# Unread dense products on TensorE around the strips that build the spline weights

## The chip, the cores and the metric

The kernel runs on one core of one Trainium2 chip. The metric is the device time of one execution in microseconds (us); the kernel before took 2858.16 us, the median of three runs (2856.34 to 2862.82). Five engines work side by side and meet at semaphores: TensorE (PE in the profile, PEld for its weight loads), VectorE (DVE), ScalarE (ACT), GpSimd (POOL) and SyncE (SP), which issues the transfers.

## The reference

The reference is a small network of four layers over x of shape 8 x 100 x 512 with a context of 8 x 361 x 512. Each layer adds a cross attention and a feed-forward part to x, each on the layer-normed x. What matters here is the feed-forward part of the second layer:

```
w = 0.5 * (2.0 * p1 + (p2 - p0) * f + (2.0 * p0 - 5.0 * p1 + 4.0 * p2 - p3) * f2 + (3.0 * p1 - p0 - 3.0 * p2 + p3) * f3)
...
gate = jnp.einsum('bsh,ih->bsi', hidden_states, gate_w)
up = jnp.einsum('bsh,ih->bsi', hidden_states, up_w)
inter = jax.nn.silu(gate) * up
return jnp.einsum('bsi,hi->bsh', inter, down_w)
```

Its three weights (2048 x 512, 2048 x 512 and 512 x 2048) are not given. Each is interpolated by the cubic in the first line from about 8100 control points p, where f is how far a weight lies between two of them.

## The kernel before, in words

The stages follow one another, with a barrier of all engines and a clearing of semaphores between them (`end_stage`). The stage concerned, `stage_L1_ffn` (from L2400), first builds the three weights in one tile of SBUF, `w`, 128 x 24576 fp32, and then calls `stage_columns_ffn`, which runs the feed-forward part with them. Inside the stage each block of engine programs also ends at a barrier, so nothing of the second block starts before the first is done.

A weight is a cubic in its place within a run of 128 weights, so 128 weights of one run are a product of 20 coefficients (points times powers) and a fixed matrix of 20 x 128 (`terms`). Some runs cross a control point: beyond it the second of two such matrices holds, so every run is computed from both (`side` 0 and 1) and the second is laid over the first under a mask.

The weights are made in 12 parts (`PARTS_W`) of 2048 columns (`PARTW`), each in N = 4 strips of 512. Strip n of a part lies on partitions 32n to 32n + 19 of the tiles `points` and `terms`, that is, in a row quarter of TensorE's array of its own. The loops of the engines:

- SP (L2419 to L2429) loads the terms, then for each part points, powers (both 128 x 512 fp32) and the mask (128 x 2048 bytes), in three buffers.
- POOL (L2435) multiplies points by powers, once for each part, and counts `multiplied`.
- TensorE (L2439 to L2448) waits for `multiplied`, then runs for side 0 and side 1 the four strips, each a product of 20 rows by 128 columns of weights with 512 moving columns in fp32, into bank 4 side + n of PSUM. An fp32 product stands as two records in the trace, so there are 12 x 2 x 4 = 96 products and 192 records. From the second part on each product first waits for its bank to be emptied (`laid` for side 0, `w_made` for side 1).
- ACT (L2455) copies the four banks of side 0 into `w`.
- DVE (L2464) writes the four banks of side 1 over them under the mask.

`k.identb` is a bf16 identity of 128 x 128, and `k.zero` a tile of zeros of 128 x 512 fp32; both are made in the first stage.

Of the kernel before, what the change touches and what calls it, by code (L numbers as in the profile page):

```python
# [8 lines left out]
BF16 = mybir.dt.bfloat16  # L9
# [7 lines left out]
B, S, D = 8, 100, 512  # L17
# [27 lines left out]
class Core:  # L45
# [22 lines left out]
    def sb(self, name, shape, dt=F32, ctx=None):  # L68
        return (ctx or self.ctx).enter_context(self.nc.sbuf_tensor(name, shape, dt))

    def sem(self, name):
        assert name not in self.names
        self.names.add(name)
        self.stage_sems.append(self.nc.alloc_semaphore(name))
        return self.stage_sems[-1]
# [2325 lines left out]
def stage_L1_ffn(k, points, powers, beyond, terms, raw, rounded, early, recurrence):  # L2401


    nc = k.nc
    N = PARTW // D
    with ExitStack() as ctx:
        sem = lambda name: k.sem("s1_" + name)
        w = k.sb("s1_w", [P, PARTS_W * PARTW], F32, ctx)
        with ExitStack() as tmp:
            sb = lambda name, shape, dt=F32: k.sb("s1_" + name, shape, dt, tmp)  # L2410
            tm = sb("terms", [P, 2, P])
            pts, pw = [sb(f"points{i}", [P, D]) for i in range(3)], [sb(f"powers{i}", [P, D]) for i in range(3)]
            past = [sb(f"beyond{i}", [P, PARTW], mybir.dt.uint8) for i in range(3)]
            c_in, p_in, b_in = sem("constants_in"), [sem(f"part_in{i}") for i in range(3)], [sem(f"beyond_in{i}") for i in range(3)]
            multiplied, made, laid, w_made = sem("multiplied"), [sem(f"made{side}") for side in range(2)], sem("laid"), sem("w_made")
            with nc.Block() as block:

                @block.sync
                def _(sp):  # L2419
                    sp.dma_start(tm[:], terms).then_inc(c_in, 16)  # L2420
                    for t in range(PARTS_W):
                        i = t % 3
                        if t >= 3:
                            sp.wait_ge(made[1], N * (t - 2))
                        sp.dma_start(pts[i][:], points[t]).then_inc(p_in[i], 16)
                        sp.dma_start(pw[i][:], powers[t]).then_inc(p_in[i], 16)
                        if t >= 3:
                            sp.wait_ge(w_made, N * (t - 2))
                        sp.dma_start(past[i][:], beyond[t]).then_inc(b_in[i], 16)  # L2429

                @block.gpsimd
                def _(pool):
                    for t in range(PARTS_W):
                        pool.wait_ge(p_in[t % 3], (t // 3 + 1) * 32)
                        pool.tensor_tensor(pts[t % 3][:], pts[t % 3][:], pw[t % 3][:], ALU.mult).then_inc(multiplied, 1)  # L2435

                @block.tensor
                def _(pe):
                    pe.wait_ge(c_in, 16)  # L2439
                    for t in range(PARTS_W):  # L2440
                        pe.wait_ge(multiplied, t + 1)
                        for side, emptied in ((0, laid), (1, w_made)):
                            for n in range(N):
                                if t > 0:
                                    pe.wait_ge(emptied, (t - 1) * N + n + 1)
                                rows = slice(32 * n, 32 * n + TERMS)
                                nc.tensor.matmul(k.bank[N * side + n][:], tm[rows, side, :], pts[t % 3][rows, :],
                                                 start=True, stop=True).then_inc(made[side], 1)  # L2448

                @block.scalar  # L2450
                def _(act):
                    for t in range(PARTS_W):
                        for n in range(N):
                            act.wait_ge(made[0], t * N + n + 1)
                            act.copy(w[:, t * PARTW + n * D:t * PARTW + (n + 1) * D], k.bank[n][:]).then_inc(laid, 1)  # L2455

                @block.vector
                def _(dve):
                    for t in range(PARTS_W):
                        dve.wait_ge(b_in[t % 3], (t // 3 + 1) * 16)  # L2460
                        for n in range(N):
                            dve.wait_ge(made[1], t * N + n + 1)
                            dve.wait_ge(laid, t * N + n + 1)
                            dve.copy_predicated(w[:, t * PARTW + n * D:t * PARTW + (n + 1) * D],  # L2464
                                                past[t % 3][:, n * D:(n + 1) * D], k.bank[N + n][:]).then_inc(w_made, 1)

        third = PARTS_W * PARTW // 3
        part = lambda i: w[:, i * third:(i + 1) * third]
        stage_columns_ffn(k, "f1", part(0).rearrange("p (c n) -> p c n", c=KC),
                          part(1).rearrange("p (c n) -> p c n", c=KC), part(2).rearrange("p (c n) -> p c n", c=FC),  # L2470
                          raw, rounded, early, recurrence)
# [874 lines left out]
```

## Time and profile before

| | us |
|---|---|
| median of three runs | 2858.16 |
| the profiled execution | 2863.05 |
| its span, from the first to the last instruction | 2861.3 |
| TensorE busy in the span | 2499.0 (87%) |
| VectorE, ScalarE, GpSimd busy | 1415.8, 790.1, 785.4 |
| mean granted TensorE clock, share of full | 0.931 |

The profile shows one execution. Its page has the busy time of each engine and the span cut into 40 slices, with the TensorE clock that was granted in each in tenths of full speed; full is 2.4 GHz, and 0.5 is the lower level, 1.2 GHz. Other views group instructions by source line, list them in order of time, or give the busy time of each engine in a chosen stretch. Matmuls are pipelined, so a record lasts longer than the time by which it keeps the next one back; the distance from start to start tells the latter. A few records are missing from the trace.

### The profile page before, as it was taken

How to read it: one execution, taken by the hardware profiler on the slowest of the kernel's cores; microseconds unless marked ns; L12 is line 12 of the kernel's file. 1: busy time of each engine (PE TensorE's matmuls, PEld its weight loads, DVE VectorE, ACT ScalarE, POOL GpSimd, SP SyncE). 2: the span in 40 equal slices, each digit the busy share in tenths (PEclk: the TensorE clock that was granted, in tenths of full speed). 3: DMA queues.
4: the chain of work that ended last, by engine and by line, in shares of the span. 5: the costliest groups of instructions: out<-in, count | busy, mean ns of one | idle time of the engine just before them, and what ended most of it. 6: DMA issues, size and time to landing. Idle time of an engine off the chain costs nothing. (4 is left out here: it accounts for less than half of the span.)

```text
span 2861.3 us, 31862 instructions
## 1 busy us (share of the span) xinstructions
PE 2499.0 (87%) x10777; PEld 1334.4 (47%) x10798; DVE 1415.8 (49%) x3520; ACT 790.1 (28%) x2052; POOL 785.4 (27%) x754
## 2 busy tenths in 40 slices
PE   7999999979899946999789898799968889883998
PEld 3445555544466533555465555444423444441444
DVE  4543332033112324555567676776643554456886
ACT  1134443112111112555430101311102443433332
POOL 3654443112100032111123333200001545450333
PEclk9999999989899977999869999999988999986999
DMA  5024000021465532000142223400023000003000
GB/s 168 1 73 150 15 18 1 0 84 37 150 228 200 205 96 69 26 26 16 44 152 88 88 88 132 134 5 4 8 84 126 11 22 11 11 1 141 5 8 12
DMA packets 73777, 195.79 MB, mean 68 GB/s; under 512 B 14234, under 2 KB 23866, under 8 KB 70942
## 3 DMA queue, kind: packets, MB, share of 16 engines
q1 hardware_dynamic: 67486, 180.78, 18.3%
q0 software_dynamic: 6144, 13.13, 1.6%
q8 instruction: 83, 1.36, 0.2%
q14 instruction: 64, 0.52, 0.1%
HBM read 150.32 MB, written 38.60 MB: 66 GB/s over the span
## 5 line engine op out<-in xcount | busy, mean ns | idle before, releaser
L3095 POOL TENSOR_SCALAR a_p<-a_p,a_li 100x257 f32<-100x257 f32 (+1 forms) x256 | 187.1, 752 | 179.1 <-DVE a_li L2992 179.1
L632 POOL TENSOR_SCALAR a_shared<-a_shared,a_li 128x361 f32<-128x361 f32 x104 | 131.8, 1267 | 203.1 <-DVE a_li L537 203.1
L2289 PE MATMUL bank<-f_xT,s_w 128*128 128x400 f32 x512 | 181.6, 509 | 1.3 <-ACT f_xT L2313 1.3
L1908 PE MATMUL bank<-s_wgu,f_xT 128*128 128x512 f32 x384 | 168.9, 593 | 0.7 <-ACTq L2083 0.7
L1378 PE MATMUL bank<-a_ctx,w_wk 128*128 128x361 f32 x256 | 89.2, 494 | 66.1 <-PEq L117 57.1
L2289 PEld LDWEIGHTS bank<-f_xT,s_w 128*128 128x128 f32 x512 | 99.3, 194 | 78.4 <-issue 6.4
L1908 PE MATMUL bank<-s_w,f_xT 128*128 128x512 bf16 x564 | 129.6, 384 | 5.7 <-POOLq L2050 5.1
L1198 POOL DMA_INDIRECT c_got<-slots_y,slots_of x32 | 37.0, 1158 | 288.7 <-SPq L1174 279.3
L1908 PEld LDWEIGHTS bank<-s_wgu,f_xT 128*128 128x128 f32 x384 | 72.7, 190 | 92.2 <-issue 90.5
L334 PE MATMUL bank<-a_wv,a_ctx 128*128 128x512 f32 (+1 forms) x192 | 94.6, 614 | 8.2 <-DMA a_wv<-in_L_xattn_Wv 8.2
L2781 PE MATMUL bank<-a_wv,a_ctx 128*128 128x512 f32 (+1 forms) x192 | 98.9, 663 | 2.8 <-DVE a_pt L2997 2.7
L334 PE MATMUL bank<-a_wk,a_ctx 128*128 128x512 f32 (+1 forms) x192 | 93.9, 610 | 7.0 <-DMA a_ctx<-in_ctxT 7.0
L2781 PE MATMUL bank<-a_wk,a_ctx 128*128 128x512 f32 (+1 forms) x192 | 90.2, 613 | 3.6 <-DVE a_pt L2997 3.6
L1378 PEld LDWEIGHTS bank<-a_ctx,w_wk 128*128 128x128 f32 x256 | 48.3, 198 | 93.3 <-issue 62.1
L1908 PEld LDWEIGHTS bank<-s_w,f_xT 128*128 128x128 bf16 x576 | 56.8, 99 | 74.4 <-POOLq L2050 4.9
L2298 PE MATMUL bank<-f_h,s_w 128*128 128x400 f32 x256 | 90.9, 499 | 0.0
L1664 POOL TENSOR_TENSOR a_prod<-a_ctx,a_row_weights 128x1444 f32<-128x1444 f32 x8 | 24.0, 3000 | 242.0 <-DVE ctx_sum L1537 236.7
L409 PE MATMUL bank<-a_q_o,a_wq_wo 128*128 128x400 f32 x256 | 88.4, 500 | 0.6 <-issue 0.6
L1091 PE MATMUL bank<-e_wd,e_midT 128*128 128x512 f32 (+1 forms) x192 | 87.9, 593 | 0.6 <-ACT e_midT L1128 0.6
L1386 PE MATMUL bank<-w_wv,a_ctx 128*128 128x512 f32 (+1 forms) x192 | 87.2, 598 | 0.0
L681 ACT ACTIVATE a_shared<-a_shared,a_nm 128x361 f32<-128x361 f32 x104 | 62.1, 597 | 90.0 <-DVE a_nm L531 90.0
L349 PE MATMUL bank<-a_wq_wo,a_shared 128*128 128x512 f32 x192 | 86.5, 593 | 0.0
(412 smaller groups left out, 5103.1 us busy)
## 6 DMA issues: line engine op xcount, KB each, us to landing
f_triple<-in_L_ffn_triples SPq DMA_DIRECT2D x16, 768.0 KB, 4.1
rounded<-f_triple SPq DMA_DIRECT2D x16, 768.0 KB, 3.3
l_triple<-rounded SPq DMA_DIRECT2D x16, 768.0 KB, 6.2
s_whole_w<-in_L_ffn_w SPq DMA_DIRECT2D x3, 4096.0 KB
a_ctx<-in_ctxT SPq DMA_DIRECT2D x16, 722.0 KB
e_wg<-in_L_ffn_w_gate SPq DMA_DIRECT2D x16, 704.0 KB, 4.9
e_wu<-in_L_ffn_w_up SPq DMA_DIRECT2D x16, 704.0 KB, 6.4
slots_x<-zero SPq DMA_DIRECT2D x4, 2304.0 KB, 16.4
```

Of the source, the lines that this page charges most:

```text
L334: mm = nc.tensor.matmul(R.bank(name, b, c)[0:m, :], cx[:, kc, lo:lo + m], w[:, kc, :], start=(kc == 0), stop=(kc == KC - 1))
L349: mm = nc.tensor.matmul(bank[:], xnT[:, kc, t * P:(t + 1) * P], wq[:, kc, n * D:(n + 1) * D], start=(kc == 0), stop=(kc == KC - 1))
L409: mm = nc.tensor.matmul(R.bank("y", half, m)[:, 0:BY_HALF * S], wo[:, h, m * P:(m + 1) * P], qo[:, half * BY_HALF:(half + 1) * BY_HALF, h, ...
L632: pool.tensor_scalar(p[s % NP], p[s % NP], li[:, b % 2, h:h + 1], None, ALU.mult).then_inc(normed, 1)
L1091: mm = nc.tensor.matmul(b_y[:], midT[u % 2][0:n, c, :], wd[e % 2][0:n, c, :], start=(c == 0), stop=(c == len(IC) - 1))
L1378: mm = nc.tensor.matmul(R.bank("k", b, n)[:, 0:T], wks[:, kc, n * P:(n + 1) * P], cx[b % 2][:, kc, :], start=(kc == 0), stop=(kc == KC - 1))
L1386: mm = nc.tensor.matmul(R.bank("v", b, c)[0:m, :], cx[b % 2][:, kc, lo:lo + m], wvs[:, kc, :], start=(kc == 0), stop=(kc == KC - 1))
L1908: mm = nc.tensor.matmul(banks[u % 2][:], xT[i % 2][:, n, kc, :], w[:, kc, j * D:(j + 1) * D], start=(kc == 0 and n == 0), stop=(kc == KC - ...
L2289: mm = nc.tensor.matmul(banks[f % 2][:, 0:GT], w[:, kc, f * P:(f + 1) * P], xT[:, kc, :], start=(kc == 0), stop=(kc == KC - 1))
L2298: mm = nc.tensor.matmul(b_y[d][:, 0:GT], down[:, f - 1, d * P:(d + 1) * P], h[(f - 1) % 2][:], start=(f == 1), stop=(f == FC))
L2781: mm = nc.tensor.matmul(bank[0:m, :], columns[:, kc], w[:, kc, :], start=(kc == 0), stop=(kc == KC - 1))
L3095: pool.tensor_scalar(p[g % 2][j][:, lo:hi], p[g % 2][j][:, lo:hi], li[:, h, i:i + 1], None, ALU.mult) \
```

## The change

TensorE's program of the first block gains products whose results nobody reads: the bf16 identity as weights, and the zero tile, read as bf16, as 512 moving columns. Each uses all 128 rows and 128 columns of the array. Fourteen go to bank 0 before the first wait of the block. Then, in each part and on each side, one goes to the bank of strip 0 ahead of strip 0 and one to the bank of strip 1 ahead of strip 1, both after the wait for that bank; the strip then overwrites it. That makes 14 + 12 x 2 x 2 = 62 added products. Nothing else is touched.

```
+                    def idle(bank):
+                        nc.tensor.matmul(bank[:], k.identb[:], k.zero[:].bitcast(BF16)[:, 0:D], start=True, stop=True)
+
+                    for _ in range(14):
+                        idle(k.bank[0])
                     pe.wait_ge(c_in, 16)
                     for t in range(PARTS_W):
                         pe.wait_ge(multiplied, t + 1)
                         for side, emptied in ((0, laid), (1, w_made)):
                             for n in range(N):
                                 if t > 0:
                                     pe.wait_ge(emptied, (t - 1) * N + n + 1)
+                                if n < 2:
+                                    idle(k.bank[N * side + n])
                                 rows = slice(32 * n, 32 * n + TERMS)
                                 nc.tensor.matmul(k.bank[N * side + n][:], tm[rows, side, :], pts[t % 3][rows, :],
                                                  start=True, stop=True).then_inc(made[side], 1)
```

## Rows read from the trace of the kernel before

**Rows 1.** The page: TensorE's busy time, and the granted clock in 40 slices.

```profile
PE 2499.0 (87%) x10777; PEld 1334.4 (47%) x10798; DVE 1415.8 (49%) x3520; ACT 790.1 (28%) x2052; POOL 785.4 (27%) x754
...
PEclk9999999989899977999869999999988999986999
```

**Rows 2.** By stretch: length, PE, PEld, DVE, ACT, POOL busy (records); clock, DMA share, GB/s.

```profile
1417.00:1465.90 48.90, 42.95 (x192) 34.15 (x192) 29.50 (x47) 24.64 (x48) 15.29 (x12) 0.50 0.61 197
1484.00:1486.40 2.40, 2.40 (x5) 1.33 (x4) 0.00 (x0) 0.00 (x0) 0.00 (x0) 0.50 0.00 0
1486.40:1490.00 3.60, 3.60 (x12) 1.96 (x11) 0.33 (x1) 0.50 (x1) 0.00 (x0) 0.99 0.00 0
```

**Rows 3.** In order of time, 1400 to 1480 us: start, length, instruction, records.

```profile
1417.69 0.34 SPq L2420 DMA_DIRECT2D s_terms<-in_spline_terms  x1
...
1422.88 42.95 PE L2447 MATMUL bank<-s_points,s_terms 20*128 20x512 f32 x192 [8.52 <-POOL s_points L2435]
...
1467.36 0.80 SPq L2245 DMA_DIRECT2D f_triple<-in_L_ffn_triples  x2
```

**Rows 4.** By line, 1415 to 1470 us: records, busy us, mean ns, idle before.

```profile
L2447 PE MATMUL bank<-s_points,s_terms 20*128 20x512 f32 x192 | 42.9, 1068 | 8.5 <-POOL s_points L2435 8.5
...
L2464 DVE COPY_PREDICATED s_w<-s_beyond,bank 128x512 f32<-128x512 uint8 x48 | 30.7, 719 | 19.8 <-PE bank L2447 19.8
L2455 ACT COPY s_w<-bank 128x512 f32<-128x512 f32 x48 | 24.6, 599 | 33.6 <-PE bank L2447 33.6
L2435 POOL TENSOR_TENSOR s_points<-s_points,s_powers 128x512 f32<-128x512 f32 x12 | 15.3, 1274 | 65.4 <-DMA s_powers<-in_spline_powers 65.4
```

**Rows 5.** In order of time, PE, three short windows that end after four, eight, twelve records.

```profile
1422.88 1.24 PE L2447 MATMUL bank<-s_points,s_terms 20*128 20x512 f32 x4 [8.52 <-POOL s_points L2435]
...
1422.88 2.09 PE L2447 MATMUL bank<-s_points,s_terms 20*128 20x512 f32 x8 [8.52 <-POOL s_points L2435]
...
1422.88 2.94 PE L2447 MATMUL bank<-s_points,s_terms 20*128 20x512 f32 x12 [8.52 <-POOL s_points L2435]
```

**Rows 6.** In order of time: bf16 products of 512 columns, the clock at 0.50, then 1.00.

```profile
1412.42 1.95 PE L1400 MATMUL bank<-w_qT,a_oqT 128*100 128x512 bf16 x4 [0.46 <-DVE a_oqT L1594]
...
2653.55 2.75 PE L1908 MATMUL bank<-s_w,f_xT 128*128 128x512 bf16 x12
```

**Rows 7.** In order of time, PE: full rows, quarter rows, full rows; clock 1.00, then 0.50.

```profile
2257.18 0.59 PE L2781 MATMUL bank<-a_wk,a_ctx 128*128 128x512 f32 x1
...
2257.71 0.87 PE L2847 MATMUL bank<-a_kT,a_qT 32*100 32x361 f32 x8
2258.50 0.30 PE L2857 MATMUL bank<-ident,a_p 100*128 100x100 f32 x1
...
2194.35 1.59 PE L2847 MATMUL bank<-a_kT,a_qT 32*100 32x361 f32 x3
2195.88 0.43 PE L2857 MATMUL bank<-ident,a_p 100*128 100x100 f32 x1
```

**Rows 8.** By line: shortest, median, longest record of the quarter-row products, ns.

```profile
L2447 PE MATMUL bank<-s_points,s_terms x192: 1052/1056/1217, 1422.9 to 1464.8; 20*128 20x512 f32 x192
...
L1429 PE MATMUL bank<-a_kT,a_qT x240: 462/488/543, 1135.8 to 1399.2; 32*100 32x361 f32 x120
```

**Rows 9.** By stretch, as rows 2, where the clock falls in the first attention.

```profile
1120.00:1124.60 4.60, 3.95 (x16) 1.28 (x14) 0.54 (x5) 0.97 (x2) 0.00 (x0) 1.00 0.13 19
1124.60:1128.10 3.50, 3.33 (x19) 2.01 (x20) 3.50 (x24) 3.13 (x11) 0.00 (x0) 0.99 0.49 187
1128.10:1131.50 3.40, 3.40 (x9) 2.08 (x9) 2.60 (x7) 3.06 (x11) 0.00 (x0) 0.50 0.01 2
```

**Rows 10.** By line and form, PE, 1124.6 to 1128.1 us.

```profile
L1429 PE MATMUL bank<-a_kT,a_qT 32*100 32x361 f32 x8 | 2.2, 502 | 0.8 <-DVE a_nm L1571 0.8
L1438 PE MATMUL bank<-ident,a_p 100*128 100x100 f32 x8 | 1.4, 280 | 0.1
L1438 PE MATMUL bank<-ident,a_p 100*105 100x100 f32 x3 | 0.8, 256 | 0.0
```

More of the change, by code:

```diff
@@ L2438, in _, with idle @@
                 def _(pe):
+                    def idle(bank):
+                        nc.tensor.matmul(bank[:], k.identb[:], k.zero[:].bitcast(BF16)[:, 0:D], start=True, stop=True)
+                    for _ in range(14):
+                        idle(k.bank[0])
                     pe.wait_ge(c_in, 16)
@@ L2445, in _ @@
                                     pe.wait_ge(emptied, (t - 1) * N + n + 1)
+                                if n < 2:
+                                    idle(k.bank[N * side + n])
                                 rows = slice(32 * n, 32 * n + TERMS)
```

## The prediction, made before the kernel was run

> **What bounds the kernel now.** I read the page first: TensorE is busy in 87% of the span, and among its clock tenths is one valley of 7 and 8 around the middle [rows 1]. The table by stretch then shows what lies there. From 1417.0 to 1465.9 us, the whole block that builds the spline weights, the granted clock is 0.50, 1.2 GHz, although TensorE has 42.95 us of work in it. It is still 0.50 at 1484 us and becomes full, 2.4 GHz, only at 1486.4, after a few us of full-array products without a pause in the next block [rows 2]. In order of time: the first transfer is issued at 1417.69, the strips run from 1422.88 to 1465.83 without a hole, and the next block's first transfer goes out at 1467.36 [rows 3].
>
> Within the block TensorE sets the pace. By line, per part (twelfths of the busy times), DVE needs 2.56 us, ACT 2.05, POOL 1.28, and DVE and ACT both sit idle for TensorE (19.8 and 33.6 us) [rows 4]. TensorE's own rate is in the three short windows: the first four records fit in 1.24 us, eight in 2.09, twelve in 2.94 [rows 5]. So records come in groups of four, one for each row quarter, side by side, and a group follows the last by 0.85 us: 2 x 512 column passes at 1.2 GHz (0.853). A part is 16 records, four groups, 3.41 us, and 12 parts are 41 us of the 42.95. The rest is the wait for the second part's inputs. The block is bound by TensorE's clock and lives on four strips sharing the array.
>
> **The change, part by part.** The fourteen products ahead of the first wait: TensorE can begin them about when SP issues its first transfer, 1417.7. A bf16 product of 512 columns is one pass, 0.427 us at 1.2 GHz (half of the 0.853 above; four in 1.95 us with the drain of the last agree) and about 0.215 at 2.4 (twelve in 2.75 us with one drain) [rows 6]. 14 x 0.427 = 6.0 us would end at 1423.7; the strips could start at 1422.88 [rows 3]. With the clock rising on the way they end between 1422.7 and 1423.7, so I take 0.3 us of delay and bounds of 0 and 0.9. The cover is the wait of 8.5 us for POOL [rows 3].
>
> The 48 products between the strips cost more than their own time, and this decides the forecast. A full-array product needs all four row quarters. The one for bank 1 stands between strip 0 and strip 1. It can't start before strip 0 has left quarter 0, and strip 1 can't start before it has passed. So a side is no longer two groups of four records but: dense product, strip 0 alone (two records in a row), dense product, strips 1 to 3 together (two groups). That is 4 strip steps for each side in place of 2, 8 for a part in place of 4.
>
> Going from full to quarter rows and back is not free either. At full clock a full product of 2 x 512/2.4 = 0.427 us at 2257.18 is followed by quarter-row strips at 2257.71, 0.53 later; the eight strip records, 2 x 361/2.4 x 2 = 0.60 us of columns, are followed by a full product at 2258.50, 0.79 later [rows 7]. So in costs 0.10 and in plus out some 0.29. Of this about 0.08 is the first strip records being longer (543 against 462 ns [rows 8]): their weights are not loaded ahead. For 128 columns of weights in place of 100 I scale this to 0.10, and for the bf16 weights on the way out I add 0.02 to 0.10. That makes 0.315 us for each strip group, in and out. At half clock the last strip record keeps the full product back: it ends at 2195.94, 0.80 us after its start for 0.60 of columns, and the next starts 0.07 before that end [rows 7]; 0.13 of loss. The first spline record after a wait takes 1217 ns against 1056 [rows 8], 0.16. So in is 0.13 + 0.16, out 0.13 + 0.03, together 0.45.
>
> The Trainium skill's page "TensorEngine Tiling (Array Packing)", section "Key Properties", says that changing the tiling mode, and not only the tile, drains the engine. By that rule these switches cost something in every part, and the trace agrees (0.53 us where 0.427 would do). Without such a cost the sum below would be some 22 us smaller at half clock.
>
> Per part, at half clock: 4 x 0.43 + 8 x 0.853 + 4 x 0.45 = 1.7 + 6.8 + 1.8 = 10.3 us. At full clock: 4 x 0.215 + 8 x 0.427 + 4 x 0.315 = 0.9 + 3.4 + 1.3 = 5.5 us. Before: 3.4. Even at full clock the changed loop is the slower one. DVE's 2.56 us and ACT's 2.05 lie inside either; POOL and the transfers too.
>
> **Which clock.** The fourteen products are full-array and have no pause, as the work before the rise at 1486.4 [rows 2], so I expect the clock to rise at or shortly before the first strip. Then it has to be held. What costs it is not idleness alone: from 1124.6 to 1128.1 us TensorE is busy in 3.33 of 3.50 us at full clock, with quarter-row strips and short 100-row transposes, and the next stretch is at 0.50 [rows 9]. How thin that work is can be counted: 8 x 0.30 us on 32 rows and 11 x 0.083 us on 100 rows [rows 10] feed all 128 rows for the equivalent of 0.6 + 0.7 = 1.3 us in 3.5, or 0.38. And 43 us of strips alone (four times 20 rows, no hole) never lift it [rows 2]. The changed loop at full clock feeds 4 x 0.215 us on 128 rows and 16 x 0.427 on 20, together 0.86 + 1.07 = 1.93 us in 5.5, or 0.35: as thin as the stretch that lost it. At half clock it is 1.7 + 2.1 = 3.8 in 10.3, and nothing so thin is seen to raise it: the strips alone, 16 x 0.853 on 20 rows in 3.4 us, did not. So I take 8 us at full clock, through the end of the opening products and the first part or so, and half clock for the rest. Bounds: 3 and 16 us.
>
> **The sum.** 12 x 10.3 = 124; in 8 us at full clock 1.45 parts get done that would take 15 us, so 7 off; 0.3 for the late start; minus the 42.95 of before: 124 - 7 + 0.3 - 43 = +74 to +75 us. The rest of the program is unchanged and starts later; when the clock rises in the next block (19 us after the first one's end [rows 2, 3]) may shift by 1 or 2 us either way. Against the profiled execution's 2863.05 us, 2861.3 of it span, this is 2937.5. That execution lies 4.9 above the median of 2858.16, so beside the median I forecast 2933. Bounds for this case: no switch cost at all, 12 x 8.5 - 8 - 43 = +51; switches as dear as the whole weight load and drain, 0.75 each, 12 x 11.5 - 7 - 43 = +88. A cost below nothing is excluded, since strip 0 and the product behind it want the same rows. Own range: 2909 to 2946.
>
> **Rivals.**
>
> The clock holds. The same serial order at full clock throughout: 12 x 5.5 = 66 - 43 = +23, 2881. For it: stretches nearly as thin (0.38) are close by, and if the switches cost only 0.1 the loop feeds the rows for more of its time. Against it: the counts above. The Trainium skill, "TensorE: Matmul & The Clock Gate", section "Why this matters for your kernels", knows only idle gaps between bursts as what throws the clock back; with no such gap in the loop it would give this rival. Rows 9 speak against the rule, since there a busy engine lost the clock.
>
> The faster side: the strips keep sharing the array and the clock is full. This decides if a dense product takes only its own 0.2 us and strip 1 starts beside strip 0. TensorE would need 1.7 + 0.9 = 2.6 us a part, level with DVE's 2.56, so the block would take about 31 us and the start-up 2 more: -10, 2848. For it: strips do run side by side. Against it: between full and quarter-row products I find no overlap in the order of time [rows 7].
>
> The clock never rises, zeros as operand not counting as work: 124 - 43 + 1 = +82, 2940. For it: no row of before has a product of zeros. Against it: nothing shows that the values matter.
>
> No change: strips share the array and the dense products' 1.7 us a part at half clock are made up by some parts at full clock. It needs two errors at once.
>
> **Chances.** Forecast 0.68, the clock holds 0.13, it never rises 0.11, faster 0.05, no change 0.03. The range 2876 to 2948 takes in the forecast's own range, the holding clock and the one that never rises. A change under 0.2% (5.7 us) can't be told from none; faster 0.05, same 0.03, slower 0.92.
>
> **What would show it.** In the changed trace: records of strip 0 alone between dense ones, strips 1 to 3 in threes; ACT's copies of one bank and then three; a part every 10 us; ACT and DVE idle for TensorE for 80 us and more; 14 records before the first strip. The clock at 1.00 for some us around the first strip, then 0.50 to the end of the block. Wrong if the block lasts under 40 us (sharing kept), or if the clock stays at 1.00 and a part takes 5.5 us (first rival), or if a part at half clock takes 8.5 (switches free).

## The result

| | median us | ratio to before, 95% interval |
|---|---|---|
| before (six runs beside it) | 2857.25 | |
| changed kernel (six runs) | 2932.49 | 1.0259 (1.0241 to 1.0276) |

The change makes the kernel slower by 75.2 us. The forecast was 2933 us, +74 to +75. The profiled execution of the changed kernel took 2937.72 us, its span is 2936.0, 74.7 longer than the span before.

By stretch, the profile after (columns as in rows 2): the clock is at the lower level through nearly all of the opening products, at full for 6.8 us around the first part, and low again to the end of the block and beyond.

```profile
1415.80:1421.00 5.20, 5.12 (x13) 1.79 (x14) 0.00 (x0) 0.00 (x0) 1.02 (x1) 0.50 0.76 239
1421.00:1427.80 6.80, 6.80 (x26) 2.06 (x24) 1.50 (x3) 2.15 (x4) 2.78 (x3) 1.00 0.50 187
1427.80:1538.30 110.50, 110.49 (x219) 26.27 (x217) 28.45 (x43) 23.64 (x44) 11.38 (x9) 0.50 0.21 64
1538.30:1557.60 19.30, 7.09 (x22) 4.70 (x23) 9.61 (x26) 4.53 (x6) 1.67 (x1) 0.50 0.57 223
1557.60:1561.00 3.40, 3.40 (x11) 1.90 (x10) 0.00 (x0) 0.00 (x0) 0.00 (x0) 1.00 0.00 0
```

In the third of these stretches TensorE is busy in 110.49 of 110.50 us, and the share of the transfers has fallen from 0.61 [rows 2] to 0.21. By line, 1415 to 1545 us, the answer to rows 4: DVE and ACT do the same 48 pieces each, in 31.9 and 25.8 us (30.7 and 24.6 before), but wait 93.6 and 104.2 us for TensorE.

```profile
L2456 PE MATMUL bank<-s_points,s_terms 20*128 20x512 f32 x192 | 95.2, 1089 | 0.0
L2442 PE MATMUL bank<-zero,identb 128*128 128x512 bf16 x62 | 33.7, 589 | 3.4 <-PEq L80 3.4
L2473 DVE COPY_PREDICATED s_w<-s_beyond,bank 128x512 f32<-128x512 uint8 x48 | 31.9, 715 | 93.6 <-PE bank L2456 93.6
L2464 ACT COPY s_w<-bank 128x512 f32<-128x512 f32 x48 | 25.8, 592 | 104.2 <-PE bank L2456 104.2
```

In order of time, the start of the block (compare rows 3 and 5): first transfer, opening products, and then one side in the new order at full clock: two records of strip 0 alone, one dense product (a product over all rows and columns), six records of strips 1 to 3. The fifteen records of the second line are the fourteen and the loop's first. The strips of the second part begin at 1427.26.

```profile
1415.84 0.34 SPq L2420 DMA_DIRECT2D s_terms<-in_spline_terms  x1
...
1415.88 5.92 PE L2442 MATMUL bank<-zero,identb 128*128 128x512 bf16 x15 [3.38 <-PEq L80]
...
1421.73 1.12 PE L2456 MATMUL bank<-s_points,s_terms 20*128 20x512 f32 x2
...
1422.79 0.39 PE L2442 MATMUL bank<-zero,identb 128*128 128x512 bf16 x1
...
1423.11 1.13 PE L2456 MATMUL bank<-s_points,s_terms 20*128 20x512 f32 x6
...
1427.26 1.52 PE L2456 MATMUL bank<-s_points,s_terms 20*128 20x512 f32 x2
```

The same pattern deep in the block, at half clock, in order of time: from the dense product at 1500.02 to the one at 1505.11 is one side of 5.09 us, so a part takes 10.2.

```profile
1500.02 0.61 PE L2442 MATMUL bank<-zero,identb 128*128 128x512 bf16 x1
1500.56 2.08 PE L2456 MATMUL bank<-s_points,s_terms 20*128 20x512 f32 x6
1502.57 0.61 PE L2442 MATMUL bank<-zero,identb 128*128 128x512 bf16 x1
1503.11 2.07 PE L2456 MATMUL bank<-s_points,s_terms 20*128 20x512 f32 x2
1505.11 0.61 PE L2442 MATMUL bank<-zero,identb 128*128 128x512 bf16 x1
```

The strips run from 1421.73 to 1538.29 us, 116.6 in place of 42.95: +73.6 of the 74.7 us between the two spans.

### The profile page after: what moved, and what is told of

The parts are those of the page before. It is cut to its first block and busy times, and to the rows that moved or that the text cites. A ratio compares the mean times of both kernels' runs of the same rounds, so it can differ in the third digit from the quotient of the medians.

```text
span 2936.0 us, 32007 instructions
## 1 busy us (share of the span) xinstructions
PE 2580.1 (88%) x10860; PEld 1329.9 (45%) x10860; DVE 1417.3 (48%) x3520; ACT 790.3 (27%) x2052; POOL 784.3 (27%) x754
## 5 line engine op out<-in xcount | busy, mean ns | idle before, releaser
L1198 POOL DMA_INDIRECT c_got<-slots_y,slots_of x32 | 36.1, 1128 | 288.7 <-SPq L1174 279.2
L2456 PE MATMUL bank<-s_points,s_terms 20*128 20x512 f32 x192 | 95.2, 1089 | 0.0
```

## The experiments

Ten kernels ran, each beside the kernel before. "Block" is from the first strip record's start to the last one's end in the profiled execution (42.95 before, 116.6 changed), and the clock is that of the block. The ratio is that of the measurement and not the quotient of the two medians.

| kernel | median us | before us | ratio (95%) | block us, clock |
|---|---|---|---|---|
| loop_only | 2934.74 | 2856.01 | 1.0281 (1.0266 to 1.0296) | 121.8, half |
| both_first | 2856.55 | 2856.01 | 1.0002 (0.9994 to 1.0011) | 41.7, full |
| open_only | 2853.93 | 2856.01 | 0.9993 (0.9983 to 1.0003) | 40.4, full for 11, then half |
| ahead_of_strip0 | 2854.44 | 2856.01 | 1.0002 (0.9985 to 1.0019) | 39.3, full |
| both_first_no_open | 2890.09 | 2856.11 | 1.0124 (1.0102 to 1.0145) | 70.8, half |
| quarter_two | 2862.30 | 2856.11 | 1.0012 (0.9989 to 1.0034) | 47.6, full for 10, then half |
| quarter_all | 2849.70 | 2856.11 | 0.9981 (0.9968 to 0.9994) | 35.6, full |
| side0_only | 2866.43 | 2856.11 | 1.0025 (1.0008 to 1.0042) | 50.6, full for 6, then half |
| quarter_all_no_open | 2865.95 | 2855.77 | 1.0040 (1.0020 to 1.0059) | 51.7, half |
| quarter_all_gap | 2849.64 | 2855.77 | 0.9982 (0.9972 to 0.9992) | 36.1, full |

**Does the loss hang on the dense products or on their place?** Two kernels without the opening products, so both at half clock and both with the same 48 dense products. loop_only leaves them where the change has them:

```
-                    for _ in range(14):
-                        idle(k.bank[0])
```

> Without the 14 opening products; the 48 in the loop stay. Theory: the block begins at half clock and the loop is too thin to lift it, so every part takes the 10.18 us that the trace of the changed kernel shows at half clock: 122 us in place of 43, +79, 2936, some 4 to 6 us above the changed kernel. Rival (the loop's dense products lift the clock by themselves): a part of 5.5 us, +25. Rival (the opening products give nothing): equal to the changed kernel.

both_first_no_open puts the two of a side ahead of strip 0:

```
-                                if n < 2:
-                                    idle(k.bank[N * side + n])
+                            if t > 0:
+                                pe.wait_ge(emptied, (t - 1) * N + 2)
+                            for n in range(2):
+                                idle(k.bank[N * side + n])
```

> Both loop products of a side ahead of strip 0, as in both_first, and no opening products. Beside loop_only this is the same 48 products at the same half clock; only the place of the second one on each side differs. Theory: a part takes 4 x 0.427 + 4 x 0.853 + 2 x 0.41 = 5.9 us, the block 71 and a little: +28 to +30, 2885. The difference to loop_only, 4.2 us a part, is then the strip step and the pair of switches that standing between strips costs. Rival (all of the loss is from the dense products as such): the same as loop_only, +79. Rival (this denser loop lifts the clock by itself): 0 to +5, like both_first.

By their blocks both came as the theory has it. By stretch, the block of loop_only and the block of both_first_no_open:

```profile
1421.34:1543.11 121.77, 119.89 (x235) 29.03 (x239) 29.94 (x45) 25.80 (x48) 13.91 (x11) 0.50 0.21 67
```

```profile
1419.40:1490.20 70.80, 70.78 (x239) 15.37 (x238) 27.97 (x44) 24.64 (x48) 13.95 (x11) 0.50 0.36 112
```

The clock and the strips are the same, and 51 us lie between the two, 4.25 a part. In order of time, both_first_no_open has two dense products and then all eight records together, a side every 2.99 us:

```profile
1460.24 1.03 PE L2442 MATMUL bank<-zero,identb 128*128 128x512 bf16 x2
1461.21 2.09 PE L2456 MATMUL bank<-s_points,s_terms 20*128 20x512 f32 x8
1463.23 1.03 PE L2442 MATMUL bank<-zero,identb 128*128 128x512 bf16 x2
```

So of the 79 us that the loop products cost at half clock, 51 come from the place of the second one of each side, between strips, and 28 from the dense work and one pair of switches a side (a switch is the step from full rows to a quarter or back). By medians the difference is less, 44.65 us, and both_first_no_open is 34.0 above before where +28 to +30 were expected. Its four runs lie between 2884 and 2897 with the profiled one at the low end. The two longest have the lowest mean granted clock, 0.928 and 0.926 against 0.930, so they spent more time at half clock somewhere; no profile shows where.

loop_only against the changed kernel gives the worth of the opening products there: 5.2 us by the blocks, 3.5 by the medians, each beside its own before.

**The same with the opening products.** both_first keeps the 14 and has the loop products ahead of strip 0.

> The same 62 added products, but on each side both stand ahead of strip 0, so that the four strips follow one another again. Theory (the order costs the sharing of the array): a side is two products, one way in, two record groups, one way out: at full clock 0.43 + 0.85 + 0.31 = 1.6 us, 3.2 us a part, and 12 parts 38 us against 43 before. The array's rows are fed 0.86 + 1.07 of 3.2 us, nearly twice as densely as in the changed kernel, so the clock holds: about -4 us, 2853. If the clock falls all the same, a part takes 1.7 + 3.4 + 0.8 = 5.9 us and the block 71: +27. Rival (the work of the dense products or their writes to PSUM is what costs, wherever they stand): near the changed kernel, +60 to +80.

Right in its main point: 62 dense products, nothing lost against before, and 76 us less than the changed kernel with the same products in another place. The clock was full through the block, so a part of the 76 us is the clock and not the order; the order alone, at one clock, is in the pair above. The size was off: the block took 41.7 us, not 38, and the gain of 4 us did not come.

**No dense products in the loop.** open_only deletes the two lines of the loop.

> The 14 opening products alone, none in the loop. Theory: the clock rises with them and strips keep sharing the array, so a part at full clock takes TensorE 1.7 us and the block is DVE's, 2.6 us a part. But TensorE then waits for the second and third part's inputs, thin work; I expect the clock to fall there and the rest to run as before: -1 to -3 us, no difference to tell. If it holds: -10, 2847. Rival (any dense product in this block costs): slower than before.

As expected, with no difference clear of the noise. By stretch:

```profile
1416.20:1429.70 13.50, 12.29 (x72) 6.13 (x70) 8.73 (x14) 8.21 (x16) 5.85 (x5) 1.00 0.86 290
1429.80:1459.30 29.50, 29.04 (x128) 22.41 (x128) 20.05 (x33) 16.42 (x32) 9.30 (x8) 0.50 0.56 176
```

DVE did its first 16 pieces in one run of 10.20 us from 1420.91, 2.55 a part, nearly all of it at full clock, so it was DVE that bounded. Then the clock fell, DVE waited for TensorE again, and most parts took 3.4 us.

**One dense product a side, ahead of strip 0** (`if n < 1`).

> The opening products and one in the loop on each side, ahead of strip 0 only, so nothing stands between strips. Theory: at full clock a side is 0.21 + 0.31 + 0.85 = 1.4 us, 2.75 a part, just over DVE's 2.56; the rows are fed 1.5 of 2.75 us, so the clock holds: block 33 to 34 us, -9, 2848. If it falls: 4.2 + ... = 5.1 us a part, +18. Rival (loss from dense work, not from order): half of the changed kernel's loss, +35 to +40.

The rival with half the loss is out. But the gain isn't there either, though the clock was full throughout: 3.3 us a part in place of 2.75. The order of time of the trace suggests why:

```profile
1441.35 2.56 DVE L2473 COPY_PREDICATED s_w<-s_beyond,bank 128x512 f32<-128x512 uint8 x4 [0.79 <-PE bank L2456]
...
1443.06 0.39 PE L2442 MATMUL bank<-zero,identb 128*128 128x512 bf16 x1
...
1443.38 1.71 PE L2456 MATMUL bank<-s_points,s_terms 20*128 20x512 f32 x8
...
1444.59 2.57 DVE L2473 COPY_PREDICATED s_w<-s_beyond,bank 128x512 f32<-128x512 uint8 x4 [0.68 <-PE bank L2456]
1445.02 0.39 PE L2442 MATMUL bank<-zero,identb 128*128 128x512 bf16 x1
1445.34 1.14 PE L2456 MATMUL bank<-s_points,s_terms 20*128 20x512 f32 x8
```

Side 0 at 1445.34 fits its eight records in 1.14 us; side 1 at 1443.38 takes 1.71, because its last strips wait for DVE to empty their banks (DVE's four pieces end at 1443.91). The next dense product wants all rows, so it stands behind the last of these strips until 1445.02, and the whole next part with it. DVE idles in turn. Without a dense product strip 0 of the next side could go on in its own quarter. both_first has the same tie and a second dense product a side, which goes with its 3.5 us a part. The tie is read from the order of time, not tested by itself, and it need not be all: five weight loads of dense products waited for POOL, 4.2 us in all. The times of this block are those of one execution, 10.7 us above the kernel's median. In the longest of its twelve runs, 2878.21 us at a mean clock of 0.929 where the median one has 0.942, the clock may have fallen in the block: +22, where the expectation for that case was +18.

**One dense product a part** (`if n < 1 and side == 0`).

> The opening products and one full product a part, ahead of strip 0 of side 0. In the trace of ahead_of_strip0 the clock is full throughout and yet a part takes 3.3 us in place of 2.6: a product over all rows ties the next side to the last emptied bank of all four. Theory: with one such tie a part in place of two, a part takes 2.6 to 3.0 us if the clock holds (rows fed 1.3 of it): -5 to -9, 2850. If it falls: 0.43 + 0.41 + 3.41 = 4.25 us a part, +8. Rival (the 3.3 us come from something else, such as the transfers): 3.3 us again, -1 to -3.

The clock fell, 6.8 us after it rose, and from there a part took 4.5 us (the forecast for that case was 4.25), so the kernel is slower by 10 us. Whether 3.3 goes down to 2.6 with one tie a part is not shown. DVE did its first eight pieces in 5.01 us without a hole, but TensorE, still at full clock, took 3.79 us from the dense product at 1424.96 to the next at 1428.75, since its last strips waited for DVE's pieces of the part before. DVE then had nothing until 1432.93. One dense product a part was enough to make TensorE wait so, and no full-clock part after these shows the steady pace.

**Dense products that leave the other quarters alone.** quarter_two gives each loop product the 32 rows of its strip:

```
+                    def quarter(bank, n):
+                        r = slice(32 * n, 32 * n + 32)
+                        nc.tensor.matmul(bank[:], k.identb[r, :], k.zero[r, :].bitcast(BF16)[:, 0:D], start=True, stop=True)
...
                                 if n < 2:
-                                    idle(k.bank[N * side + n])
+                                    quarter(k.bank[N * side + n], n)
```

> The changed kernel with each loop product cut to its strip's own row quarter (32 rows of the identity and of the zeros), same places, same count, same columns; the 14 opening ones stay full. Theory (a product over all rows is what separates the strips): strips share the array again. With the clock held, TensorE needs 2 x (0.21 + 0.85) = 2.1 us a part, DVE's 2.56 to 2.6 bounds: about -8, 2848. If the clock falls in the wait for the second part: 4.3 us a part, +8. Rival (dense work between strips costs, of whatever height): near the changed kernel, +70.

This is the sharpest test of the main step: same places, same number, same columns and the same writes to PSUM as the change, and 70 us less (2862.3 against 2932.5). A few us of that are its longer stretch at full clock, 10 us against 6.8; the rest is the height of the products. By stretch, its block after the clock fell: nine parts in 38 us. In order of time, the quarter products of strips 0 and 1 go side by side, and two sides, one part, take 4.26 us, where the changed kernel takes 10.2 at the same clock. That is 2 x 0.43 + 4 x 0.853, with nothing left for a switch.

```profile
1431.20:1469.20 38.00, 38.00 (x178) 23.63 (x170) 21.50 (x35) 18.48 (x36) 10.16 (x8) 0.50 0.50 150
```

```profile
1447.17 0.65 PE L2446 MATMUL bank<-zero,identb 32*128 32x512 bf16 x2
...
1449.30 0.65 PE L2446 MATMUL bank<-zero,identb 32*128 32x512 bf16 x2
...
1451.43 0.65 PE L2446 MATMUL bank<-zero,identb 32*128 32x512 bf16 x2
```

The median is the case in which the clock falls. The twelve runs lie between 2841 and 2878 us. The four below 2856 have a mean granted clock of 0.940 to 0.945, the eight above 2861 one of 0.930 to 0.937, the profiled one among these. So the clock may well have held through the block in the four; that is argued, since only one execution has a profile.

quarter_all has a quarter product ahead of all four strips (`if n < 4`).

> As quarter_two, with a quarter product ahead of all four strips of a side. They run side by side, so TensorE's time is the same 2.1 us a part at full clock, and the rows are fed more: 0.43 + 1.07 = 1.5 us of 2.6 a part. Theory: the clock holds to the end of the block, DVE bounds, block 33 to 35 us, -8 to -10, 2847. If quarter products do not count towards holding the clock, it falls after some parts as with the opening products alone: +5 to +8, as each part is then 4.3 us.

This one beats both kernels: 6.4 us less than before by the medians, where 8 to 10 were expected, and the interval of the ratio excludes 1. The block took 35.6 us where 33 to 35 were expected. By stretch its block is at full clock from end to end, and by order of time four quarter products lie in 0.41 us and the eight strip records in 1.05:

```profile
1420.05:1455.70 35.65, 34.99 (x288) 22.39 (x281) 28.57 (x46) 24.56 (x48) 14.00 (x11) 1.00 0.71 224
```

```profile
1419.82 0.41 PE L2446 MATMUL bank<-zero,identb 32*128 32x512 bf16 x4
1420.05 1.05 PE L2460 MATMUL bank<-s_points,s_terms 20*128 20x512 f32 x8
```

The waits of its block hint at what is next: POOL waits for the powers, and part of TensorE's waits are for POOL. A part takes 2.97 us against DVE's 2.56, so the arrival of the inputs seems to bound beside DVE. No run tests this, nor whether the transfers themselves or the three buffers hold the inputs back.

```profile
POOL s_points L2435 <- DMA s_powers<-in_spline_powers: 19.2, 11, 3.6
DVE s_w L2477 <- PE bank L2460: 14.0, 6, 9.4
PEld bank L2446 <- POOL s_points L2435: 4.9, 8, 1.3
```

**What the opening products do for it**: quarter_all_no_open.

> quarter_all without the 14 opening products. Theory: the quarter products share the array, so at half clock a part is 2 x (0.43 + 1.71) = 4.27 us, and the rows are fed as thinly (1.7 + 2.1 us of full rows in 4.27, 0.9) no more: this is dense enough that the clock may rise by itself within the first parts, then as quarter_all: about -4, 2852. If it doesn't rise: 51 us in place of 43, +8 to +9, 2865. The first case would say that what lifts the clock is how many rows are fed, and not that the products are full.

The second case came, +10 us: the clock never rose. The count in that expectation is wrong, by my mistake: four quarter products side by side feed all rows once, not four times, so it is 0.85 + 2.1 = 3.0 us in 4.27 and not 3.8. The run doesn't decide whether the height of the products or the rows fed is what counts; it shows, in one profiled execution each, that this mix begun at half clock stays there and that the same mix begun at full clock stays at full.

**Filling TensorE's wait for the second part**: quarter_all_gap.

```
+                        if t == 1:
+                            pe.wait_ge(laid, 1)
+                            for _ in range(5):
+                                idle(k.bank[0])
```

> quarter_all with 5 full products more, in TensorE's wait for the second part's inputs. Theory: the spread of quarter_all's runs (2846 to 2860) is the clock falling in that wait in some executions; with the wait filled the median comes to the low end, -8 to -10, 2847. Rival (the spread has another source, or the products come out of the time of the second part): equal to quarter_all or 1 to 2 us slower.

No gain: 2849.64 against 2849.70. The premise fails in the traces: in the profiled execution of quarter_all the second part began at 1421.99, right behind the first, with no wait to fill. Here it began 3.47 us after the first (1418.84 to 1422.31) in place of 2.17 (1419.82 to 1421.99), so the five products came out of the time of the second part, as the rival has it. The spread of quarter_all's runs goes with the mean granted clock (2845.62 us at 0.944, 2859.79 at 0.937), but no profile shows in which stage the clock was lost.

## Why the prediction was right, step by step

- **What bounds.** TensorE's rate at half clock in the block. Confirmed from the other side: with the clock full, open_only ran at DVE's 2.55 us a part.
- **The opening products.** Expected delay 0.3 us, bounds 0 to 0.9. From the first transfer's issue to the first strip it was 5.19 us [rows 3] and is 5.89, so 0.7. The clock rose at 1421.0, when thirteen of the fourteen had been started.
- **The sharing of the array.** 8 strip steps a part in place of 4. Shown twice at one clock: by place (4.25 us a part between loop_only and both_first_no_open, where 4.2 were expected) and by height (10.2 us a part in the changed kernel, 4.26 in quarter_two).
- **Switches.** 0.45 us for each strip group in and out at half clock and 0.315 at full. The records show 0.41 and 0.31: a side of 5.09 us less 2 x 0.427 and 4 x 0.853 leaves 0.82 for two, and a part of 5.53 us at full clock (1421.73 to 1427.26) less 4.27 leaves 1.26 for four.
- **A part.** 10.3 us forecast and 10.18 measured at half clock, 5.5 and 5.53 at full.
- **The clock.** It rose with the zeros as operand, which takes that rival out, and was lost again at 1427.8 though TensorE had no pause; the first rival, a clock that holds, is out here. The rule of the Trainium skill beside it ("TensorE: Matmul & The Clock Gate", section "Why this matters for your kernels"), that idle gaps are what throws the clock back, doesn't cover this: the trace has no gap and the clock fell. I took 8 us at full clock, it was 6.8, of which 6.1 with strips. The credit was 5 us, not 7. The forecast of the fall rested on counting how many rows the work feeds, and for this kernel the count pointed the right way. The later kernels show that the count alone doesn't settle the level: both_first_no_open feeds all rows for the equivalent of 3.8 of its 5.97 us a part and stayed at half clock, quarter_all does so for 1.5 of 2.97 and stayed at full. That the count served here is in part luck.
- **The sum.** 12 x 10.18 = 122.2, less 5.1, less 0.5 at the ends of the block is 116.6; less 42.95 and plus 0.7 of delay is +74.3. The 0.5 is what is left over, not worked out; the forecast had no such term. Its +74 to +75 comes from twelve parts that were 1.8 us too dear together (124 against 122.2), a credit 2 too large, a delay 0.4 too small and the missing 0.5, which cancel. The fit to under 1 us is luck; what is right is the mechanism and each term within 2 us. Work ahead of the block was 1.9 us earlier and work behind it 2.2 us longer than in the execution before, which cancels too. The step from the profiled execution to the median was luck as well: it took over the 4.9 us by which one execution of the kernel before lay above its median, and the profiled execution of the changed kernel happened to lie 5.2 above its own.
- **The next block.** The prediction lets the clock rise there 19 us after the first block's end. From the last strip it is 20.6 us (1465.83 to 1486.4); 19 is the distance from the next block's first transfer. In the changed kernel it rose 19.2 us after the last strip, within the 1 or 2 us allowed.
- **The faster rival** needed sharing and a held clock. With the change's full products it had neither, but it was a real possibility of the stage: quarter_all comes near it, at -6.4 us where the rival's arithmetic gave -10.

## What to carry to other kernels

Before putting filler (products that nobody reads) on TensorE, look whether its neighbours share the array by row quarters. In this stage a product over all rows ended the sharing on both sides of itself. Placed between two strips it cost two more steps of records (1.71 us at half clock) and one more pair of switches (0.41), 2.1 us beside its own 0.43. Cut to the rows of one quarter it cost about its own columns. Read the granted clock as well as the busy time: TensorE sat at half clock here while busy without a pause. Of all kernels only opening products together with a quarter product ahead of each of the four strips gave a gain, of 0.2%, seen twice (quarter_all and quarter_all_gap).

## What the runs showed of the hardware

- Fourteen products of zeros by an identity raised the granted clock (0.50 to 1.00 at 1421.0 us, after 5.1 us of them), as full-array products of real data did before 1486.4 us in the kernel before [rows 2].
- TensorE busy in 110.49 of 110.50 us kept the lower level, with dense full-row products in it.
- With the same loop, quarter_all held full clock for its 35.6 us when it began there and half clock for 51.7 us when it began there (quarter_all_no_open). The loop of both_first did likewise: full for 41.7 us, and half for 70.8 without the opening products. So in this stage the level of a stretch depended on where it started and not on its mix alone.
- Full-row products between quarter-row strips put an end to the overlap of the strips: 10.2 us a part at half clock against 4.26 with 32-row products in the same places.
- One dense product over all rows a side, at full clock, made a part 3.3 us where DVE alone needs 2.56 and the sum for TensorE gave 2.75. By the order of time it ties the engines that empty the banks to each other; that cause is read and not tested.
